# Summing squares over channels: TensorE transposes and a VectorE sum in place of matmuls with a column of constants

## The reference

```python
def rmsnorm(x, w, eps=EPS):
    xf = x.astype(jnp.float32)
    inv = jax.lax.rsqrt(jnp.mean(xf * xf, axis=-1, keepdims=True) + eps)
    return (xf * inv).astype(x.dtype) * w
...
xn = rmsnorm(x, norm_w)
q = (xn @ wq).reshape(B, T, N_HEADS, HEAD_DIM)
...
attn = jax.nn.softmax(scores.astype(jnp.float32), axis=-1).astype(q.dtype)
return residual + out @ wo
```

## Time and profile before

| what | value |
|---|---|
| time of the kernel, 3 runs | 2079.6 to 2081.34 us, median 2081.07 us |
| profiled execution, span from first to last instruction | 2080.3 us |
| TensorE busy | 2042.1 us (98%) |
| VectorE busy | 1389.7 us (67%) |
| ScalarE busy | 966.4 us (46%) |
| GpSimd busy | 644.7 us (31%) |
| narrow layers in the trace | from about 793 us (L1) and about 1697 us (L3) |

### The profile page before, as it was taken

The page is one execution under the profiler, slowest core; times in us unless marked ns, Lnnn a source line. Parts: engine busy times, 40 slices in busy tenths (PEclk is TensorE's granted clock), DMA queues, the critical chain, the costliest instruction groups (busy, mean ns, idle before and its releaser), DMA issues.

```text
span 2080.3 us, 31294 instructions
## 1 busy us (share of the span) xinstructions
PE 2042.1 (98%) x11546; PEld 1764.4 (85%) x11546; DVE 1389.7 (67%) x2408; ACT 966.4 (46%) x1814; POOL 644.7 (31%) x519
## 2 busy tenths in 40 slices
PE   8999999999999998999999999999999989999998
PEld 8999988888888887788888888888888877888887
DVE  5322365775577557788888676557755775888886
ACT  3222354544355344555555454335443553555553
POOL 1000043311232244454443341223112533444441
PEclk9999999999999999999999999999999999999999
DMA  7889742222122222343333332212221232333332
GB/s 190 174 178 206 189 96 67 67 65 78 51 72 69 71 70 78 86 105 98 90 94 94 104 97 64 75 56 67 65 78 51 72 90 66 80 87 89 86 72 83
DMA packets 262537, 191.02 MB, mean 92 GB/s; under 512 B 197522, under 2 KB 199986, under 8 KB 259826
## 3 DMA queue, kind: packets, MB, share of 16 engines
q1 hardware_dynamic: 262386, 189.03, 35.6%
HBM read 132.66 MB, written 56.26 MB: 91 GB/s over the span
## 4 chain that ended last, share of the span: by engine, by line
PE 89%; DVE 6%; DMA 1%; ACT 1%; issue 1%; SPq 1%; POOL 0%; DVEq 0%; ACTq 0%; POOLq 0%
PE acc_bank L878 11%; PE acc_bank L261 8%; PE acc_bank L263 8%; PE acc_bank L262 8%; PE q_bank L836 8%; PE q_bank L840 8%; PE q_bank L838 8%; PE t_bank L858 7%; PE ctx_bank L261 3%; PE ctx_bank L262 3%; PE ctx_bank L263 3%; PE s_bank L799 2%; PE s_bank L261 2%; PE s_bank L796 2%; PE s_bank L802 2%; PE s_bank L263 2%
## 5 line engine op out<-in xcount | busy, mean ns | idle before, releaser
L1313 POOL TENSOR_TENSOR prob<-prob,rinv 128x1232 f32<-128x1232 f32 x128 | 288.5, 2254 | 1026.2 <-DVE rinv L1197 1026.2
L1055 ACT ACTIVATE q_s<-q_bank 128x512 fp32r<-128x512 f32 x192 | 115.0, 599 | 499.1 <-PE q_bank L840 494.8
L878 PE MATMUL acc_bank<-pT_s,vals_s 128*128 128x512 f32 x1024 | 337.8, 415 | 0.0
L1155 DVE TENSOR_REDUCE mx<-s_bank 128x4 f32<-128x308 f32 x512 | 240.2, 469 | 122.1 <-PE s_bank L263 63.2
L836 PE MATMUL q_bank<-x_s,w_s 128*128 128x512 f32 x768 | 318.9, 415 | 0.0
L840 PE MATMUL q_bank<-x_s,w_s 128*128 128x512 f32 x768 | 313.4, 408 | 0.0
L838 PE MATMUL q_bank<-x_s,w_s 128*128 128x512 f32 x768 | 312.8, 407 | 0.0
L261 PE MATMUL acc_bank<-o_s,w_s 128*128 128x512 f32 x752 | 303.6, 404 | 1.6 <-DVE o_s L1188 1.6
L263 PE MATMUL acc_bank<-o_s,w_s 128*128 128x512 f32 x752 | 296.7, 395 | 0.0
L262 PE MATMUL acc_bank<-o_s,w_s 128*128 128x512 f32 x752 | 296.7, 395 | 0.0
L1159 DVE TENSOR_TENSOR prob<-s_bank,mx 128x308 f32<-128x308 f32 x512 | 245.1, 479 | 27.4 <-DVE mx L1155 1.4
(11 more groups left out here) (107 smaller groups left out, 4095.5 us busy)
## 6 DMA issues: line engine op xcount, KB each, us to landing
stream<-x_back SPq DMA_DIRECT2D x128, 256.0 KB, 2.6
x_front<-stream SPq DMA_DIRECT2D x96, 256.0 KB, 3.3
x_back<-stream SPq DMA_DIRECT2D x96, 256.0 KB, 3.7
kvw_raw<-kvw SPq DMA_DIRECT2D x17, 1024.0 KB, 8.3
k_scr<-k_out SPq DMA_DIRECT2D x36, 308.0 KB, 10.4
keys_s<-k_scr SPq DMA_DIRECT2D x128, 77.0 KB, 2.5
v_scr<-v_out SPq DMA_DIRECT2D x8, 1024.0 KB
vals_s<-v_scr SPq DMA_DIRECT2D x512, 6.5 KB
```

The lines of the kernel that those rows point to most:

```text
L878: mm = pe.matmul(out, w, pT_s[:, part], start=i == mine[0] and part == 2 * n and w is v[0], stop=i == mine[-1] and w is terms[-1][0] and p ...
L1155: dve.tensor_reduce(top, scored, AX_X, ALU.max).then_inc(s_max, 1)
L1313: pool.tensor_tensor(view, view, rinv[:, slot].unsqueeze(2).broadcast_to([P, TILES * GH, CTX]), ALU.mult).then_inc(p_norm, 1)
```

## The change

The four plain matmuls of `stats` become four transposes of the same blocks against `ident`, which fill the whole bank. VectorE then reduces 128x512 to 128x4 by addition, in place of the addition of a constant to 128x4. The factor and the epsilon that the column and that addition carried move to a new GpSimd instruction on 128x4, ahead of the power, with a semaphore between the two. The tile `mean_w` and its memset go.

```diff
@@ stats, TensorE
                 for t in range(TILES):
-                    mm = pe.matmul(out[:, t:t + 1], x_power[:, t * P:t * P + P], mean_w[:, :],
-                                   start=t == 0, stop=t == TILES - 1, skip_group_check=True)
+                    mm = pe.transpose(out[:, t * P:t * P + P], x_power[:, t * P:t * P + P], ident[:, :])
                 mm.then_inc(q_mm, 1)
@@ mean_squares, VectorE
                 dve.wait_ge(q_mm, item + 1)
-                dve.tensor_scalar(ms[:, gb % 2], q_bank[item % 2][:, 0:TILES], EPS * KIND_B.DH, None, ALU.add)\
-                   .then_inc(q_out, 1)
+                dve.tensor_reduce(ms[:, gb % 2], q_bank[item % 2][:, :].rearrange("q (t n) -> q t n", t=TILES),
+                                  AX_X, ALU.add).then_inc(q_out, 1)
@@ root, GpSimd
                 pool.wait_ge(q_out, plan.q[("stats", gb)] + 1)
+                pool.tensor_scalar(ms[:, gb % 2], ms[:, gb % 2], KIND_B.DH / D, EPS * KIND_B.DH, ALU.mult, ALU.add)\
+                    .then_inc(ms_scaled, 1)
+                pool.wait_ge(ms_scaled, plan.b_batch(gb) + 1)
                 pool.tensor_tensor(rstd[:, gb % 2], ms[:, gb % 2], mhalf[:, :], ALU.pow).then_inc(rstd_ready, 1)
@@ context part, GpSimd
-        pool.memset(mean_w[:, :], KIND_B.DH / D).then_inc(consts, 1)
```

More of the change, by code:

```diff
@@ L277, in __init__ @@
         self.ident = sb("ident", [P, P], F32)
-        self.mean_w = sb("mean_w", [P, 1], F32)
         self.mhalf = sb("mhalf", [P, TILES], F32)
@@ L310, in context_part @@
     banks = [early.enter_context(nc.psum_tensor(f"ctx_bank{i}", [P, 512], F32)) for i in range(8)]
-    w_A, x_s, ident, mean_w, mhalf = lasting.w_s, lasting.x_s, lasting.ident, lasting.mean_w, lasting.mhalf
+    w_A, x_s, ident, mhalf = lasting.w_s, lasting.x_s, lasting.ident, lasting.mhalf
     bias_s, bo, nw = lasting.bias_s, lasting.bo, lasting.nw
@@ L494, in link @@
             dve.wait_ge(chain, links[0])
-        dve.wait_ge(consts, 5)
+        dve.wait_ge(consts, 4)
         dve.wait_ge(setup_loaded, 16 * 4)
@@ L537, in gpsimd @@
         pool.memset(ident[:, :], 0.0).then_inc(consts, 1)
-        pool.memset(mean_w[:, :], KIND_B.DH / D).then_inc(consts, 1)
         pool.memset(mhalf[:, :], -0.5).then_inc(consts, 1)
-        pool.wait_ge(consts, 3)
+        pool.wait_ge(consts, 2)
         pool.wait_ge(cleared, 1)
@@ L622, in whole_block @@
         stage = sb("stage", [P, 2, QUARTER], F32)
-        w_s, x_s, ident, mean_w, mhalf = lasting.w_s, lasting.x_s, lasting.ident, lasting.mean_w, lasting.mhalf
+        w_s, x_s, ident, mhalf = lasting.w_s, lasting.x_s, lasting.ident, lasting.mhalf
         bias_s, bo, nw = lasting.bias_s, lasting.bo, lasting.nw
@@ L646, in whole_block @@
         acc_mm, o_hi, acc_out = map(sem, ("acc_mm", "o_hi", "acc_out"))
+        ms_scaled = sem("ms_scaled")
         rstd_ready, end_mm, end_out = sem("rstd_ready"), sem("end_mm"), sem("end_out")
```

## The result

The changed kernel takes 2066.72 us (median of 4 runs, 2066.04 to 2068.22), the one before 2080.86 us in the same comparison (4 runs): a ratio of 0.9933 [0.9919, 0.9946], 14.1 us faster. The forecast was 2078.4 us, with a range from 2075.6 to 2082.2.

The account below looks back on a forecast made before the run. TensorE, busy 98% of the span, was taken as the bound, with VectorE, GpSimd and ScalarE setting four of sixteen places. -4.50 + 1.06 + 0.8 = -2.64 us against 2081.07 gave 2078.4 us, range 2075.6 to 2082.2.

Parts of the forecast that it names:

- The time: Whole kernel: 2078.4 us forecast, 2.64 us less than before, from the work of the change alone.
- TensorE in the bodies: Batches three to eight of L1 and L3: four transposes replace eight passes, saving 0.375 us each, 4.50 us in all.
- The second batches: Second batch of L1 and L3: VectorE has no idle time, so its longer sum costs 0.53 us each, 1.06 us.
- named as a sign: Expected in the changed profile: TensorE's wait at 856 and at the beginnings 0.9 us longer (0.53 + 0.375).
- The beginnings: Where L1 and L3 begin: the exponentials end later behind VectorE's sum or GpSimd's root, costing 0.4 us each, 0.8 us.
- GpSimd: The new 128x4 instruction ahead of the power: 0.3 us with its wait, bounded by 0.10 and 1.02 us.
- VectorE: The sum over 128x512 takes 680 ns in place of an addition of 154 ns, adding 0.53 us.
- The clock: After long waits at the beginnings, one 3.4 us stretch at 1.2 GHz more or less moves the time up to 1.7 us.
- nothing more was hidden than forecast: Rival: VectorE and root terms are hidden too, or the saving counts in more places; 2075.1 or 2076.6 us, chance 0.14.
- the new instruction wasn't dear: Rival: GpSimd's new instruction costs 1.1 us and eats up the gain; 2080.4 to 2082.1 us, chance 0.16.
- transposes didn't take their record's time: Rival: transposes from `x_power` occupy TensorE for their recorded 273 ns each; slower by 5.2 us, 2086.3 us, chance 0.05.
- the clock didn't fall behind the norms of the bodies: Rival: twelve transposes in a row let the clock fall behind each norm; 27 us, 2108 us, chance 0.02.

Follow-up runs that it names:

- e2: The kernel before with the changed kernel's SBUF addresses (`mean_w` stored as fifth column of `mhalf`), work unchanged; 2067.42 us, ratio 0.9935.
- e11: The kernel before with `o_s` (and `xsq`, `x_power`, `rest`) 224 bytes higher, all else in place; 2069.16 us, ratio 0.9947.
- e5: The kernel before with `o_s` (and `xsq`, `x_power`, `rest`) 480 bytes higher, all else in place; 2068.96 us, ratio 0.9944.
- e1: The changed kernel with a 4-byte tile left where `mean_w` stood, so every address is that of before; 2078.67 us, ratio 0.9991.
- e4: The changed kernel with 32 bytes ahead of `w_s`, so that all tiles move together; 2066.06 us, ratio 0.9932.
- e8: The changed kernel's addresses, with its norm only for batches three to eight of L1 and L3, the old norm for their first two; 2063.4 us, ratio 0.9918.
- e12: The changed kernel with 32 bytes between `w_s` and `x_s`: `w_s` stays, every other tile goes 32 bytes up; 2078.42 us, ratio 0.9991.

## Why the prediction was wrong

The step that failed is the last sentence ahead of the sum: "Tiles allocated behind `mean_w` move a little in SBUF; no row prices that, and I take nothing for it." What I had no row for was given the price nothing, and no bound in the range, where the working asked for both ends. It measured 13.1 us (e2), seven times the rest of the change, 11.0 to 11.7 of them by the distance between two operands (e11, e5). Whether the other 1.5 to 2 us come from the other tiles that move is open: the intervals of e2, e5 and e11 overlap.

The remainder of the working, held against e1, where the addresses are those of before:

- **The time.** Forecast 2078.4 us; e1 took 2078.67. The difference to before is 1.9 us, with an interval that reaches from 3.7 to nothing; forecast 2.64.
- **TensorE in the bodies.** Forecast 0.375 us a batch. From the third norm of L1 to the eighth it was 892.41 to 1107.59 us before and is 891.67 to 1105.19 in e1: 1.66 us in five batches, 0.33 each; in L3 1.76, 0.35 each. Right, a tenth too large. The reading from start to start was the right one; a transpose's record lasts 273 ns, but four take 0.44 us of TensorE. By the 275 ns that the Trainium skill gives ("TensorE: Matmul & The Clock Gate", Part 4), taken as time of the engine, the kernel would have been slower; the trace agrees with it as the length of a record only.
- **The second batches.** Forecast a loss of 0.53 us. The distance from the second norm to the third grew by 0.56 and 0.60 us. Right, though TensorE's wait there grew by 0.52 us only (0.56 to 1.08) and not by the 0.9 that was named as a sign.
- **The beginnings.** Forecast 0.4 us. The distance from the first norm to the second grew by 0.55 and 0.75 us. Right in kind, too small in size. TensorE's wait is 1.0 us longer, near the 0.9 of the signs, and in L3 e1 has a second stretch of 3.4 us at the lower clock.
- **GpSimd.** Estimated 0.3 us with the wait, measured 0.28.
- **VectorE.** Worked out as 680 ns, measured 682.
- **The clock.** "One more such stretch, or one less by luck" was right. In e1 L1 begins with one of 3.4 us, as before, and L3 with two (from 1696 and from 1709.8) in place of one. In the changed kernel with its new addresses both beginnings show 6.7 us at 0.50. But the change of work isn't needed for that: e2, with the work of before, has it in L3 (1684.50 to 1691.20 at 0.50), and e4, with the work of the change, has 3.4 us in L1.
- **The work on the new addresses.** There it gives 0.7 us (2066.72 against 2067.42, e2) or 1.4 (2066.06, e4), where it gives 1.9 on the old ones. The intervals don't tell these apart. If they differ, two things in the profiles may be the reason, neither tested by itself: the longer stretches, and a wait of ScalarE where L2 begins for weights on their way. It is 1.97 us in the changed kernel, 1.95 in e4 and 1.49 in e8, but 0.67 in e2, 0.59 in e1 and 0.73 before:

```profile
1219.48 1.27 ACT L1082 ACTIVATE w_s<-stage 128x512 fp32r<-128x512 f32 x2 [1.97 <-DMA stage<-woA]
```

The rivals: nothing more was hidden than forecast (the waits at the second batches and the beginnings grew), the new instruction wasn't dear, transposes didn't take their record's time, and the clock didn't fall behind the norms of the bodies. None of them is the cause; it wasn't on the list.

## What to carry to other kernels

When an edit adds or drops a tile, the tiles behind it move, and that is a part of the change with a price of its own: keep the old addresses with a tile of the same size, or time the new ones alone, before the gain is put down to the work. Where long runs of passes are 0.234 us apart in one kernel and 0.227 in another with the same instructions, look at the distance between the two operands; and look for it in the starts of the longest run, since a group's mean can hide it. And a form that gains in the body of a layer and loses where the layer begins can be chosen batch by batch, from the idle time on the timeline.

## What the runs showed of the hardware that was not expected

- The pace of float32 passes of 128x128 by 512 depends on where the two operands stand against each other in SBUF: 0.2335 us a pass with `o_s` 32 bytes past a multiple of 256 from `w_s`, 0.2267 at a multiple, 2.9% less; with `x_s` in place of `o_s` 0.2333 and 0.2267 (e12, the changed kernel). The Trainium skill, "SBUF — State Buffer" (Operand start alignment), has an operand start at a multiple of its element's size, and says of this rule that it is about legality, not speed. All kernels here satisfy it, and by the distance alone they differ by 11 to 12 us.
- The effect needs a run of passes to come to its full size: in the changed kernel the steps of the run in L0 take 0.232 us from 401.33 to 402.72, the later ones 0.227. e1 has 0.232 in its first six as well (402.56 to 403.95). Why stays open; no run measured pairs of operands by themselves.
- A wait of TensorE of about 3.5 us can be followed by 6.7 us at the clock of 1.2 GHz, or by 3.4 us, in kernels that differ in little else (the changed kernel and e1 at the beginning of L1). 6.7 us also follow a wait of 2.51 us (e2 at the beginning of L3).
